# A decoder layer with attention, a selective scan and a ternary feed-forward: row sums broadcast through memory, quantisation from centred values, and new order tables

## The chip, the cores and the metric

One core of a Trainium2 chip runs the whole layer in one launch. The metric is the device time of that launch in microseconds. Engines are PE (TensorE), DVE (VectorE), ACT (ScalarE), POOL (GpSimd) and SP (SyncE, which here only issues DMAs).

## The reference, cut to what matters

Four sequences (B = 4) of L = 512 rows and DM = 512 columns pass through three residual blocks; all is float32.

```
x = x + attention(layernorm(x))             # 16 heads of 32, rotary, causal softmax, w_o
x = x + ssm(ctx, z = layernorm(x))          # conv, silu, selective scan with 16 states, gate silu(z)
x = x + ffn(layernorm(x))                   # bitlinear, gelu, bitlinear

bitlinear(x, w):  xn = (x - mean(x)) / sqrt(var(x) + EPS)
                  gamma = max(abs(xn))                      # per row
                  x_hat = clip(xn * 128 / gamma, -128, 128) * gamma / 128
                  w_hat = sign(round(w / mean(abs(w)))) * mean(abs(w))
                  return x_hat @ w_hat.T
softmax: exp(scores - rowmax) / rowsum
ssm:     state = state * exp(delta * A) + delta * u * B_t ;  y_t = sum_n state * C_t
         delta = softplus(dt_proj(dt_lo) + bias)
```

Two facts of this matter below. Dividing a row by its own largest absolute value gives the same quotient whether or not the row was first multiplied by a positive number per row. And the softmax's row sum is one number per query row and head, while the product with V stands with the query rows along the free dimension, so the reciprocals must be spread over the 32 partitions of their head.

## The kernel before, in words

**Tiling.** A sequence is cut into 4 blocks of 128 rows, its channels into 4 blocks of 128 partitions. Attention runs in 32 slots (`p`), one for two heads of one sequence: `s` (scores, PE), its row maxima (DVE), `e` (exponentials with the row sums in `z_sum`, ACT, line 1487), `t` (transposes, PE, copies by ACT at 1503). Two slots make a group `g` of four heads, 16 groups in all: `rz` (reciprocals of the row sums) and `pv` (product with V, PE, line 1694). Line 1908 on DVE multiplies the product in PSUM with `rz_t` and writes `o_t`, from which `wo`, the output projection, is made.

**The row sums before.** DVE takes the reciprocal of 128 x 16 values (line 1900). PE multiplies each column, broadcast to 32 columns, with the identity, 16 products of 128 x 128, each of them two passes as the profile counts them (line 1731), into a bank of PSUM. ACT copies the bank to `rz_t` (line 1510). DVE's multiply at 1908 waits for that copy.

**The scan.** For each sequence and each of 16 states, ACT makes the factors (line 1377), POOL the inputs from `du` and `b_bc` (line 1248), DVE scans along the rows (lines 1795, 1803), PE transposes the result (line 1708) and DVE adds it into `y_acc` (line 1817). `b_bc` is a row of B_t broadcast to 128 partitions, loaded by SP (lines 1166, 1167) from `bc_d` in memory, two buffers. `delta` is a softplus: ACT computes relu, abs, exp and log into one scratch tile `tmp` (lines 1455 to 1461); then four instructions read it, on DVE for sequence 0 (lines 1857 to 1863), on POOL for the others (from line 1259). ACT waits with a block until the `delta` of the block before is made.

**The feed-forward.** 16 tiles of 128 rows. `xa` (statistics on DVE; on POOL six small instructions, lines 1309 to 1319, that give mean, reciprocal deviation and their product with a second deviation), `xc` (DVE subtracts the mean and multiplies with the gain, line 1985, takes the largest absolute value, 1987, and its reciprocal, 1989; POOL scales, 1325), `xt` (transposes into a high and a low part), `fc` (matmuls, line 1766, gelu by ACT, 1546, statistics by DVE, 2012), `hstat` (DVE's aggregate, 2017; three POOL instructions, 1334 to 1338), `hn` (ACT centres and scales two halves, line 1565, DVE takes their maxima, 2022), `hscale`, `hq` (DVE scales, 2035), `ht_ffn` (transposes, 1757; the low part by DVE, 2007), `proj` (line 1775) and DVE's `y_out` (2042). The tiles begin while the last sequence is still being scanned.

**What sets the order.** Each engine executes its list in order and waits on semaphores. The lists come from `plan()`, a planner that runs before the kernel is written. It takes due times for each item from tables (`STATE`, `ATTN`, `FRONT`, `TILE`, `PACE` and others), adds a weight for each engine and kind (`WEIGHT`), and with costs and needs from `follows()` picks, for the engine that can start first, the ready item that is due first. SP is one such engine, so loads and stores have one order too. It also places PSUM banks and puts transposes of no use into PE's list where PE would wait (`FILLS`, line 1582). A change of a table moves instructions on all engines.

**The start.** SP loads two blocks of x, the identity and small constants, ctx of sequence 0 with `in_w` behind it, then the residual of sequence 0 (`xr`, 1 MB, line 1189), and further loads of x. The chunks 0 and 1 of `w_ring` follow, with the rotary tables behind the first and the scan weights `xp_w` and `dt_w` behind the second.

## Time and profile before

| | |
|---|---|
| median of 3 runs | 1136.7 us (1135.46 to 1136.88) |
| the profiled execution: time, span | 1134.5 us, 1132.7 us |
| mean granted TensorE clock | 0.953 of full |
| PE busy | 1003.6 us (89%), 6034 instructions |
| DVE busy | 958.9 us (85%), 1351 |
| ACT busy | 793.3 us (70%), 1529 |
| POOL busy | 625.1 us (55%), 509 |
| DMA queue | 114.7 MB, 32.4% of 16 engines |

Busy time counts an instruction's execution, not its waits. PE's includes the fill transposes. Row forms are: `L1731 PE MATMUL out<-in shapes xcount | busy us, mean ns | idle before, with the releasers` for a group, and `engine line <- releaser: us in total, times, longest us` for a wait. SPq is the issuing of DMAs by SP. A time in a list "in order of time" is in us from the start of the span, followed by the duration.

### The profile page before, as it was taken

The page shows a single profiled execution, that of the slowest core. Times are in us where ns is not written, and L with a number is a line of the kernel's source. Part 1 is how long each engine was busy: PE and PEld are TensorE (multiplying, and loading weights), DVE is VectorE, ACT ScalarE, POOL GpSimd, SP SyncE. Part 2 cuts the span into 40 slices and gives each one's busy share as a digit, 9 for nine tenths or more (in the row PEclk, how much of TensorE's full clock was granted, in tenths as well). Part 3 has the DMA queues.
Part 4 walks back from the last instruction along what each step waited for, and adds up shares of the span by engine and source line. Part 5 has one row for each costly group of instructions (what it writes and reads, how often), then busy time and mean ns, then how long its engine had stood idle before and what let it go on. Part 6 is the DMA issues. An engine that isn't in the chain of part 4 may idle for free. (4 is left out here: it accounts for less than half of the span.)

```text
span 1132.7 us, 18945 instructions
## 1 busy us (share of the span) xinstructions
PE 1003.6 (89%) x6034; PEld 760.6 (67%) x6034; DVE 958.9 (85%) x1351; ACT 793.3 (70%) x1529; POOL 625.1 (55%) x509
## 2 busy tenths in 40 slices
PE   7998988999988999789899985887888998989997
PEld 5555666669664668556567664676767776878886
DVE  5758898996998869998986789899999999998654
ACT  4656756765786776888767696827988978984432
POOL 1369485554536796456738831569655655544401
PEclk9999999999988999899999986997899999989999
DMA  5325356364435545323555460420111110000000
GB/s 194 114 76 171 109 151 184 105 198 152 116 103 182 154 131 168 103 81 106 167 190 159 139 194 6 175 105 26 41 47 34 38 33 32 26 16 19 10 19 19
DMA packets 59360, 115.91 MB, mean 102 GB/s; under 512 B 8880, under 2 KB 13232, under 8 KB 58240
## 3 DMA queue, kind: packets, MB, share of 16 engines
q1 hardware_dynamic: 59264, 114.70, 32.4%
q8 instruction: 51, 0.84, 0.3%
q14 instruction: 45, 0.37, 0.1%
HBM read 90.42 MB, written 24.25 MB: 101 GB/s over the span
## 5 line engine op out<-in xcount | busy, mean ns | idle before, releaser
L1248 POOL TENSOR_TENSOR hb<-du,b_bc 128x1024 f32<-128x1024 f32 (+1 forms) x160 | 314.8, 1987 | 160.6 <-PE ps L1708 160.6
L1795 DVE TENSOR_TENSOR_SCAN hb<-ps,hb 128x1024 f32<-128x1024 f32 (+1 forms) x128 | 257.4, 2013 | 33.3 <-ACT ps L1377 20.0
L1377 ACT ACTIVATE ps<-delta,a_neg 128x511 f32<-128x511 f32 (+2 forms) x320 | 180.6, 600 | 79.5 <-DVE hb L1795 73.3
L1817 DVE SCALAR_TENSOR_TENSOR y_acc<-ps,ct,y_acc 128x512 f32<-128x512 f32 x256 | 181.2, 740 | 24.5 <-PE ps L1708 23.8
L1708 PE MATMUL ps<-ident,hb 128*128 128x128 f32 x1088 | 160.1, 288 | 43.8 <-DVE hb L1795 12.7
L1708 PEld LDWEIGHTS ps<-ident,hb 128*128 128x128 f32 x1088 | 127.8, 147 | 72.1 <-issue 14.2
L1487 ACT ACTIVATE p_q<-ps,m_col 128x512 f32<-128x512 f32 (+3 forms) x256 | 131.5, 530 | 20.9 <-DVE m_col L1892 12.2
L1639 PE MATMUL ps<-xn_t,w_ring 128*128 128x512 f32 x256 | 117.9, 604 | 0.8 <-DVE o_t L1908 0.6
L1766 PE MATMUL ps<-t_fc,xq_hi 128*128 128x512 f32 x256 | 106.2, 415 | 3.2 <-DVE hq_lo L2007 3.2
L1682 PE MATMUL ps<-ident,p_q 128*128 128x128 f32 x640 | 91.9, 287 | 14.4 <-ACT p_q L1487 7.2
L1503 ACT ACTIVATE p_t<-ps 128x512 f32<-128x512 f32 x160 | 88.2, 605 | 22.9 <-PE ps L1682 22.6
L1775 PE MATMUL ps<-t_pr,hq_hi 128*128 128x512 f32 x256 | 102.2, 399 | 1.9 <-DVE hq_lo L2007 1.9
L1766 PE MATMUL ps<-t_fc,xq_lo 128*128 128x512 f32 x256 | 101.9, 398 | 0.0
L1775 PE MATMUL ps<-t_pr,hq_lo 128*128 128x512 f32 x256 | 101.1, 395 | 0.0
L1892 DVE TENSOR_REDUCE m_col<-ps 128x1 f32<-128x512 f32 (+2 forms) x192 | 88.5, 501 | 8.1 <-PE ps L1667 7.0
L1682 PEld LDWEIGHTS ps<-ident,p_q 128*128 128x128 f32 x640 | 75.0, 147 | 28.5 <-ACT p_q L1487 9.2
L1663 PE MATMUL ps<-k_st,q_st 128*128 128x512 f32 (+3 forms) x256 | 76.5, 374 | 10.5 <-DVE y_acc L1817 7.8
L1639 PEld LDWEIGHTS ps<-xn_t,w_ring 128*128 128x128 f32 x256 | 46.9, 192 | 52.5 <-issue 50.0
L1582 PE MATMUL ps<-ident 128*128 128x128 f32 x478 | 67.4, 292 | 11.2 <-DMA small<-in_small 5.5
L1582 PEld LDWEIGHTS ps<-ident 128*128 128x128 f32 x478 | 59.1, 152 | 18.0 <-DMA small<-in_small 5.5
L1546 ACT ACTIVATE h_sb<-ps,fx 128x512 f32<-128x512 f32 x64 | 42.7, 686 | 30.1 <-PE ps L1766 28.5
L1565 ACT ACTIVATE h_sb<-h_sb,fh 128x1024 f32<-128x1024 f32 x32 | 38.4, 1236 | 30.9 <-POOL fh L1338 30.9
(151 smaller groups left out, 2016.5 us busy)
## 6 DMA issues: line engine op xcount, KB each, us to landing
w_ring<-in_w_attn SPq DMA_DIRECT2D x32, 512.0 KB, 3.7
qk_d<-hl SPq DMA_DIRECT2D x64, 256.0 KB
q_st<-qk_d SPq DMA_DIRECT2D x128, 128.0 KB, 2.8
b_bc<-bc_d SPq DMA_DIRECT2D x48, 256.0 KB, 3.9
k_st<-qk_d SPq DMA_DIRECT2D x64, 128.0 KB, 2.7
k_st<-qk_d SPq DMA_DIRECT2D x128, 64.0 KB, 2.3
x_in<-in_x SPq DMA_DIRECT2D x16, 256.0 KB, 2.9
raw_fc<-in_w_fc SPq DMA_DIRECT2D x4, 1024.0 KB, 9.2
```

What stands on the lines that cost most here:

```text
L1248: nc.gpsimd.tensor_tensor(piece_of(e, hi, lo).rearrange("p (a n) -> p a n", a=2), du[b % 2][:, 2 * h:2 * h + 2, lo:hi], b_bc[:, i % BC_RIN ...
L1377: ins = nc.scalar.activation(factors(j, hi, lo)[:, (hi - lo) * m + start:(hi - lo) * (m + 1)], delta[b % 2][:, et, lo + start:hi], ACT.Exp ...
L1487: ins = nc.scalar.activation(p_q[:, h, Q_AT[i]:Q_AT[i] + w], src[:, col:col + w], ACT.Exp, bias=m_col[:, i, h:h + 1], accum_out=z_sum[:, b ...
L1582: nc.tensor.transpose(bank(*item)[:, 0:P], ident[:], ident[:])
L1639: mm = nc.tensor.matmul(bank(kind, *a), w_ring[:, c % 2, d, P * half:P * half + P], xn_t[:, d, :], start=(d == 0), stop=(d == KD - 1))
L1682: mm = nc.tensor.transpose(dst[:, at:at + P], p_q[:, h, Q_AT[i] + P * jt:Q_AT[i] + P * jt + P], ident[:])
L1708: mm = nc.tensor.transpose(bank(kind, *a)[:, P * et:P * et + P], piece_of(2 * r + et // 2, hi, lo)[:, at:at + P], ident[:])
L1766: mm = nc.tensor.matmul(bank(kind, t, n), part[:, t % 2, d, :], t_fc[:, d, 512 * n:512 * n + 512], start=(d == 0 and m == 0), stop=(d == K ...
L1775: mm = nc.tensor.matmul(bank(kind, t), part[:, k, :], t_pr[:, k, :], start=(k == 0 and m == 0), stop=(k == FT - 1 and m == 1))
L1795: v.tensor_tensor_scan(h, d, h, 0.0, ALU.mult, ALU.add).then_inc(scan_done, 1)
L1817: v.scalar_tensor_tensor(out=y, in0=bank(kind, r, tb), scalar=ct[:, b % 2, tb, n:n + 1], in1=y, op0=ALU.mult, op1=ALU.add).then_inc(y_free ...
L1892: ins = v.tensor_reduce(m_col[:, i, h:h + 1], src[:, col:col + P * (i + 1)], AX.X, ALU.max, negate=True)
```

## The change

Five things are changed.

1. **Row sums.** PE's matmuls and ACT's copy for `rz` are removed. After DVE's reciprocal SP stores the 128 x 16 values to memory in another order, `[row block, head, row]`, and then loads them back into `rz_t` with four loads, each broadcast to 32 partitions. DVE's multiply waits for the loads. The planner has a due time of its own for `rzload`.
2. **Quantisation.** `xc` only subtracts the mean and takes maximum and reciprocal of the centred values; the gain goes into the scale that POOL computes for the gelu. `hn` on ACT only negates and centres (mean minus value, scale -1); the gain with a minus sign goes into the scale for `y_out`. Neither waits for POOL's gain any longer; POOL's scale instructions do.
3. **Scratch.** In sequence 0 the softplus of odd blocks uses `gate` in place of `tmp`, so each block waits for the `delta` of two blocks before.
4. **Loads.** The scan weights are loaded behind `in_w`; the first residual stands after the store of `x_dbl`.
5. **Tables.** Due times and weights for all engines are new.

```diff
 ATTN = {'stack': [-11.6],
  's': [-0.6, 1.0, 2.6, 4.2, 5.8],
- 'e': [1.2, 2.8, 4.4, 6, 7.6],
- 't': [8.4, 9.6, 9.6, 10.8, 12.0],
+ 'e': [1.2, 2.8, 4.4, 6.2, 7.8],
+ 't': [8.4, 9.6, 9.6, 9.8, 11.0],
  'pv': [14.6]}
 
...
-LAST_STATE = {'exp': [-4.8, -1.8], 'dbu': [-8.0, -5.0], 'scan': [0.9, 3], 'carry': [3.0, 6.0], 'ht': [4.6, 5.8]}
...
+LAST_STATE = {'exp': [-4.7, -1.7], 'dbu': [-8.3, -5.0], 'scan': [0.9, 3], 'carry': [11.0, 14.0], 'ht': [4.6, 5.8]}
...
-QUOTIENT = {'rz': [11.4]}
+QUOTIENT = {'rz': [21.2], 'rzload': [13.6]}
...
-PACE = {'slot': 18.0, 'ffn': 597.2, 'tile': 15, 'tail': 835.1, 'tail_step': 6.4, 'tail_load': -19.6}
...
+PACE = {'slot': 18.0, 'ffn': 597.2, 'tile': 15.5, 'tail': 822.6, 'tail_step': 13.6, 'tail_load': -18.7}
...
+def scratch_user(b, et):
+
+
+    i = ET * b + et
+    return None if i < 2 else divmod(i - 2 if b == 0 else i - 1, ET)
...
     elif kind == "xproj":
...
-        yield "pe", 3.5, [act("silu", b, ET - 1), sp("wload", 1)]
+        yield "pe", 3.5, [act("silu", b, ET - 1), sp("cload", 0)]
...
     elif kind == "e":
-        yield "act", 1.3, [dve("s", *a)] + ([pe("t", a[0] - 1, 4)] if a[0] else [])
+        p, n = a
+        yield "act", 1.3, [dve("s", *a)] + ([pe("t", p - 1, 4)] if p else []) + ([sp("rz", p // 2 - 8)] if p >= 16 else [])
...
-        yield "dve", 0.7, [pe(*item), act("rz", g)] + ([pe("wo", b - 1, 1, 1)] if b else [])
+        yield "dve", 0.7, [pe(*item), sp("rzload", g)] + ([pe("wo", b - 1, 1, 1)] if b else [])
     elif kind == "rz":
...
-        yield "pe", 0.5, [dve(*item)]
-        yield "act", 0.6, [pe(*item)] + ([dve("pv", g - 1)] if g else [])
+        yield "sp", 1.5, [dve(*item)]
+    elif kind == "rzload":
+        g, = a
+        yield "sp", 1.0, [sp("rz", g)] + ([dve("pv", g - 1)] if g else [])
     elif kind == "resid":
...
-            [pe("pv", SLOTS // 2 - 1)] if b else []
+            [pe("pv", SLOTS // 2 - 1)] if b else [sp("xproj", 0)]
...
     elif kind == "xc":
...
-        yield "dve", 1.9, [pool("xa", t), pe("xt", t - 2) if t >= 2 else dve("wo", B - 1, 1, 1)]
-        yield "pool", 1.5, [dve(*item), dve("wtot", 0)] + ([act("fc", t - 4, 3)] if t >= 4 else [])
+        yield "dve", 1.9, [dve("xa", t), pe("xt", t - 2) if t >= 2 else dve("wo", B - 1, 1, 1)]
+        yield "pool", 1.5, [dve(*item), pool("xa", t), dve("wtot", 0)] + ([act("fc", t - 4, 3)] if t >= 4 else [])
...
     elif kind == "hstat":
-        yield "dve", 0.35, [dve("fc", *a, 3)]
-        yield "pool", 1.1, [dve(*item)]
+        yield "dve", 0.35, [dve("fc", *a, 3)] + ([pool("hstat", a[0] - 4)] if a[0] >= 4 else [])
+        yield "pool", 1.1, [dve(*item), dve("wtot", 1)]
     elif kind == "hn":
-        yield "act", 1.3, [pool("hstat", a[0])]
+        yield "act", 1.3, [dve("hstat", a[0])]
...
     elif kind == "hscale":
...
-        yield "pool", 0.3, [dve(*item), dve("wtot", 1)]
+        yield "pool", 0.3, [dve(*item), pool("hstat", *a)]
...
-            before["pe", item] = before["pe", item] + [x for who in readers for x in before[who, item] if x[1] != item and (x[0], x[1][:2]) != ("pe", ("fc", item[1]))]
+            before["pe", item] = before["pe", item] + [x for who in readers for x in before[who, item] if x[1] != item and x[1][0] != "rzload" and (x[0], x[1][:2]) != ("pe", ("fc", item[1]))]
...
-        if engine == "pe" and item[0] == "dt" and scratch:
-            if scratch[-1] not in over:
+        if engine == "pe" and item[0] == "dt" and scratch_user(*item[1:]):
+            user = scratch_user(*item[1:])
+            made = delta_by(user[0]), ("delta", *user)
+            if made not in over:
...
-            at = max(at, over[scratch[-1]])
+            at = max(at, over[made])
...
-                    if c < 2:
-                        load_consts(("rotary", "scan")[c])
+                    if c == 0:
+                        load_consts("rotary")
...
+                        load_consts("scan")
...
+                elif kind == "rz":
+                    g, = a
+                    sp.wait_ge(z_ready, g + 1)
+                    sp.dma_start(rz_d[g].rearrange("i q p -> p (i q)"), z_sum[:, g // 4 % 2, g % 4].rearrange("p i q -> p (i q)"),
+                                 allow_slow_non_contiguous=True)\
+                        .then_inc(rz_stored, 16)
+                elif kind == "rzload":
+                    g, = a
+                    sp.wait_ge(rz_stored, 16 * (g + 1))
+                    if g:
+                        emptied(sp, TASK["pv", g - 1])
+                    for quad in range(4):
+                        sp.dma_start(rz_t[HD * quad:HD * quad + HD, :].rearrange("d (i p) -> d i p", p=P),
+                                     rz_d[g, :, quad].partition_broadcast(HD)).then_inc(rz_in, 16)
...
-                    nc.gpsimd.tensor_scalar(f[:, 7:8], f[:, 2:3], f[:, 3:4], None, ALU.mult).then_inc(fx_pow, 1)
+                    nc.gpsimd.tensor_scalar(f[:, 7:8], f[:, 2:3], f[:, 3:4], None, ALU.mult).then_inc(fx_gain, 1)
...
-                    nc.gpsimd.tensor_scalar(f[:, 12:13], f[:, 8:9], gam[:, 0:1], None, ALU.mult).then_inc(fx_scale, 1)
+                    pool.wait_ge(fx_gain, t + 1)
+                    nc.gpsimd.tensor_scalar(f[:, 12:13], f[:, 8:9], f[:, 7:8], gam[:, 0:1], ALU.mult, ALU.mult).then_inc(fx_scale, 1)
...
-                    nc.gpsimd.tensor_scalar(f[:, 3:4], f[:, 0:1], f[:, 2:3], -1.0, ALU.mult, ALU.mult).then_inc(fh_nmr, 1)
+                    pool.wait_ge(gam_ready, 2)
+                    nc.gpsimd.tensor_scalar(f[:, 3:4], f[:, 2:3], gam[:, 1:2], -1.0, ALU.mult, ALU.mult).then_inc(fh_gain, 1)
                 elif kind == "hscale":
...
-                    pool.wait_ge(gam_ready, 2)
-                    nc.gpsimd.tensor_scalar(f[:, 12:13], f[:, 8:9], gam[:, 1:2], None, ALU.mult).then_inc(fh_scale, 1)
+                    pool.wait_ge(fh_gain, t + 1)
+                    nc.gpsimd.tensor_scalar(f[:, 12:13], f[:, 8:9], f[:, 3:4], None, ALU.mult).then_inc(fh_scale, 1)
...
-                    if b or et:
-                        delta_made(act, *divmod(ET * b + et - 1, ET))
-                    nc.scalar.activation(tmp[:, 0, :], bank(kind, *a), ACT.Relu, bias=dt_b[:, et, :])
-                    nc.scalar.activation(tmp[:, 1, :], bank(kind, *a), ACT.Abs, bias=dt_b[:, et, :])\
+                    if scratch_user(b, et):
+                        delta_made(act, *scratch_user(b, et))
+                    s = scratch(b, et)
+                    nc.scalar.activation(s[:, 0, :], bank(kind, *a), ACT.Relu, bias=dt_b[:, et, :])
+                    nc.scalar.activation(s[:, 1, :], bank(kind, *a), ACT.Abs, bias=dt_b[:, et, :])\
...
-                    own.done(nc.scalar.activation(tmp[:, 1, :], tmp[:, 1, :], ACT.Exp, scale=-1.0))
-                    own.settle()
-                    nc.scalar.activation(tmp[:, 2, :], tmp[:, 1, :], ACT.Ln, bias=1.0).then_inc(sp_ready, 1)
+                    own.done(nc.scalar.activation(s[:, 1, :], s[:, 1, :], ACT.Exp, scale=-1.0))
+                    own.settle()
+                    nc.scalar.activation(s[:, 2, :], s[:, 1, :], ACT.Ln, bias=1.0).then_inc(sp_ready, 1)
...
+                    if b >= 2:
+                        act.wait_ge(rz_stored, 16 * (p // 2 - 7))
...
-                elif kind == "rz":
-
-                    g, = a
-                    act.wait_ge(m_full, TASK[kind, g] + 1)
-                    if g:
-                        emptied(act, TASK["pv", g - 1])
-                    nc.scalar.activation(rz_t[:], bank(kind, g), ACT.Copy).then_inc(m_free["act"], 1)
...
                 elif kind == "hn":
...
-                    act.wait_ge(fh_nmr, t + 1)
+                    act.wait_ge(fh_var, t + 1)
...
-                    nc.scalar.activation(half, half, ACT.Identity, bias=fh[:, t % 4, 3:4],
-                                         scale=fh[:, t % 4, 2:3]).then_inc(hn_done, 1)
+                    nc.scalar.activation(half, half, ACT.Identity, bias=fh[:, t % 4, 0:1], scale=-1.0).then_inc(hn_done, 1)
...
-                elif kind == "rz":
-
-                    g, = a
-                    pe.wait_ge(z_ready, g + 1)
-                    for i in range(LT):
-                        for quad in range(4):
-                            z = z_sum[:, g // 4 % 2, g % 4, i, quad:quad + 1].to_broadcast([P, HD])
-                            mm = nc.tensor.matmul(bank(kind, g)[HD * quad:HD * quad + HD, P * i:P * i + P], z, ident[:],
-                                                  start=True, stop=True)
-                    mm.then_inc(m_full, 1)
...
-                    d = delta[b % 2][:, et, :]
-                    own.done(v.tensor_scalar(d, tmp[:, 1, :], 1.0, 1.0, ALU.add, ALU.subtract))
-                    own.settle()
-                    own.done(v.tensor_tensor(d, tmp[:, 1, :], d, ALU.subtract))
-                    own.settle()
-                    own.done(v.tensor_tensor(d, d, tmp[:, 2, :], ALU.add))
-                    own.settle()
-                    v.tensor_tensor(d, d, tmp[:, 0, :], ALU.add).then_inc(delta_ready["dve"], 1)
+                    d, s = delta[b % 2][:, et, :], scratch(b, et)
+                    own.done(v.tensor_scalar(d, s[:, 1, :], 1.0, 1.0, ALU.add, ALU.subtract))
+                    own.settle()
+                    own.done(v.tensor_tensor(d, s[:, 1, :], d, ALU.subtract))
+                    own.settle()
+                    own.done(v.tensor_tensor(d, d, s[:, 2, :], ALU.add))
+                    own.settle()
+                    v.tensor_tensor(d, d, s[:, 0, :], ALU.add).then_inc(delta_ready["dve"], 1)
...
-                    emptied(dve, TASK["rz", g])
+                    dve.wait_ge(rz_in, 64 * (g + 1))
...
+                    if t >= 4:
+                        dve.wait_ge(fx_gain, t - 3)
...
                 elif kind == "xc":
...
-                    dve.wait_ge(fx_pow, t + 1)
...
-                    own.done(v.tensor_scalar(x, x2(t), f[:, 0:1], f[:, 7:8], ALU.subtract, ALU.mult))
+                    dve.wait_ge(fx_var, t + 1)
+                    own.done(v.tensor_scalar(x, x2(t), f[:, 0:1], None, ALU.subtract))
...
+                    if t >= 4:
+                        dve.wait_ge(fh_gain, t - 3)
```

Of the tables (some 100 changed numbers) only a few stand here.

## Rows read from the trace of the kernel before

**Rows 1.** stretch, us, busy PE PEld DVE ACT POOL (instructions), PEclk, DMA share, GB/s:

```profile
100.00:640.00 540.00, 492.18 (x3252) 355.36 (x3252) 464.09 (x621) 392.22 (x883) 333.46 (x190) 0.97 0.46 140
...
760.00:1000.00 240.00, 209.60 (x1073) 174.13 (x1073) 231.80 (x366) 203.18 (x303) 146.15 (x179) 0.94 0.11 33
1000.00:1060.00 60.00, 55.59 (x277) 46.36 (x276) 52.40 (x93) 32.12 (x45) 33.09 (x52) 0.94 0.04 14
1060.00:1100.00 40.00, 40.00 (x199) 33.33 (x198) 22.23 (x35) 15.49 (x23) 4.91 (x8) 1.00 0.05 21
```

**Rows 2.** the same for PE's fill transposes of line 1582 alone:

```profile
100.00:740.00 640.00, 27.88 (x200) 23.40 (x200) 0.95 0.46 141
```

**Rows 3.** groups of the page's kind: busy, mean ns, idle before and its releasers:

```profile
L1731 PE MATMUL ps<-ident,z_sum 128*32 128x128 f32 x512 | 18.4, 287 | 4.8 <-DVE z_sum L1900 3.8 <-DVE y_acc L1817 0.8
...
L1510 ACT ACTIVATE rz_t<-ps 128x512 f32<-128x512 f32 x16 | 9.6, 600 | 12.1 <-PE ps L1731 12.1
```

**Rows 4.** DMA issues (KB each, us to landing), three issues of SP:

```profile
k_st<-qk_d SPq DMA_DIRECT2D x128, 64.0 KB, 2.3
...
bc_d<-x_dbl SPq DMA_DIRECT2D x4, 32.0 KB, 2.2
...
510.43 1.70 SPq L1181 DMA_DIRECT2D k_st<-qk_d  x3
```

**Rows 5.** DMA packets and queue share, 3.5:4 us, then 36:39.2 us:

```profile
DMA packets 174, 0.07 MB, mean 149 GB/s; under 512 B 96, under 2 KB 170, under 8 KB 174
...
q1 hardware_dynamic: 174, 0.07, 83.2%
...
DMA packets 32, 0.03 MB, mean 10 GB/s; under 512 B 16, under 2 KB 16, under 8 KB 32
...
q1 hardware_dynamic: 32, 0.03, 4.7%
```

**Rows 6.** DVE in order of time: start, duration, what:

```profile
308.62 0.24 DVE L1900 RECIPROCAL z_sum<-z_sum 128x16 f32<-128x16 f32 x1
...
320.14 0.68 DVE L1908 TENSOR_TENSOR o_t<-ps,rz_t 128x512 f32<-128x512 f32 x1
...
643.47 0.24 DVE L1900 RECIPROCAL z_sum<-z_sum 128x16 f32<-128x16 f32 x1
...
650.29 0.69 DVE L1908 TENSOR_TENSOR o_t<-ps,rz_t 128x512 f32<-128x512 f32 x1 [2.12 <-PE ps L1694]
```

**Rows 7.** who waited for tile o_t's multiply: us, times:

```profile
  PE ps L1708: 9.6, 2
...
  PE ps L1682: 0.2, 1
```

**Rows 8.** the chain that ended last, in order of time, near the end:

```profile
1071.10 7.46 PE ps L1775 x32
...
1098.10 0.28 DVE fh L2017
...
1099.71 1.25 ACT h_sb L1565
```

**Rows 9.** waits from 760 to 1000 us: us in total, times, longest:

```profile
ACT h_sb L1565 <- POOL fh L1338: 10.3, 7, 2.3
```

**Rows 10.** the head in order of time:

```profile
3.52 0.43 SPq L1189 DMA_DIRECT2D xr<-in_x  x1
11.97 0.98 SPq L1134 DMA_DIRECT2D x_in<-in_x  x2
...
44.13 0.49 DVE L1857 TENSOR_SCALAR delta<-tmp 128x512 f32<-128x512 f32 x1 [2.38 <-ACT tmp L1461]
...
48.92 0.69 ACT L1455 ACTIVATE tmp<-ps,small 128x512 f32<-128x512 f32 x1 [0.89 <-DVE delta L1863]
```

**Rows 11.** waits over the whole span: us in total, times, longest:

```profile
DVE delta L1857 <- ACT tmp L1461: 4.4, 3, 2.4
...
SPq L1166 <- POOL hb L1248: 294.2, 47, 20.7
```

178 lines of the change are left out of this document (92 added, 86 removed), and 2 rows, old and new, of the table ATTN_END.

## The prediction, made before the changed kernel ran

> **What bounds the kernel now.** I read the busy time by stretch first; the reader should see that no engine is the bound everywhere. From 100 to 640 us (attention and scans) PE has 492.2 of 540 us, DVE 464.1: 91% and 86%, level once PE's fill transposes are taken off (27.9 us from 100 to 740) [rows 1, 2]. From 760 to 1000 us (last scans and FFN tiles) DVE has 231.8 of 240 us, 97%, and PE 87%: DVE bounds there. From 1060 to 1100 PE is busy all the time [rows 1], and after that two tiles end one behind the other. So a saving on PE counts before 740 us and after 1060 us, and one on waits of DVE counts between, up to DVE's idle time there: 8.2 us from 760 to 1000 and 7.6 us from 1000 to 1060 [rows 1].
>
> I then read the groups of the lines that the diff touches, and the order of time of the reciprocal and of the multiply that uses it, because what was an engine's work becomes a round trip through memory.
>
> **Part 1, the broadcast leaves PE and ACT.** Line 1731 is 512 instructions, 18.4 us of PE, and PE waited 3.8 us for the reciprocal before it; line 1510 is 16 copies, 9.6 us of ACT, and ACT waited 12.1 us for PE there [rows 3]. ACT is busy 73% of the stretch from 100 to 640 us [rows 1], so its 9.6 us are taken at nothing; the work that hides them is PE's and DVE's own. PE's 18.4 + 3.8 = 22.2 us are worth between nothing (the planner puts fills where PE waits, and DVE is as loaded) and all. I take half, as two engines of nearly equal load share the path: -11.1 us. A bank of PSUM is also held 16 times fewer; nothing shows a price for that.
>
> **Part 2, the round trip.** In its place: a reciprocal on DVE, SP's wait, a store of 128 x 16 values of 4 bytes each to scattered addresses, SP's wait for it, four loads of 64 KB written to 32 partitions each, and only then DVE's multiply at line 1908. DVE executes in order, so a late load stops scans, maxima and y_acc behind it. The reciprocal takes 0.24 us (its row stands with the gaps below). A store of 32 KB with the 16 rows of bc_d lands after 2.2 us. SP issues three loads of k_st in 1.70 us, 0.57 each, so the fourth starts 1.7 us after the first, and such a load lands 2.3 us after its issue [rows 4]. Without a price for small pieces the trip is 0.24 + 2.2 + 1.7 + 2.3 = 6.4 us. The store has 2048 pieces, 128 for each of 16 DMA engines. No row shows 4-byte data. Two rows bound a packet: the stretch with mostly small packets has 174 in 83.2% of 16 x 0.5 us, 38 ns each; the one with 2 KB packets and completion writes has 32 in 4.7% of 16 x 3.2 us, 75 ns each [rows 5]. So 128 packets add 0, 4.9 or 9.6 us, and the trip takes 6.4, 11.3 or 16.0 us. I take 11.3, the row of small packets being nearest.
>
> The Trainium skill (DMA: Bandwidth & Descriptors, Rules for kernel authors) says that a strided last dimension lowers to one descriptor per element and advises to rearrange it, which speaks against this store. The Trainium skill (same page, Bandwidth) gives about 10.5 ns per packet for a 4 KB transfer; by that, as an estimate, the store would add 1.3 us, not 4.9, and the trip would be 7.7 us. The trace has nothing of that kind, so the sum does not use it.
>
> How much time is there? Between the reciprocal and the multiply the 16 groups have 7.2, 8.4, 8.9, 11.0, 42.9, 11.5, 17.2, 17.9, 18.3, 8.2, 8.4, 9.0, 35.0, 6.8, 16.6 and 8.6 us, from the start of the one to the start of the other; the shortest and the tenth shortest of the 16 stand as rows [rows 6]. Ten are under 12 us and add up to 88.0. A trip of 11.3 us overruns nine of them (76.5 in sum) by 9 x 11.3 - 76.5 = 25 us; one of 6.4 us none; one of 16.0 us all ten by 72 us. Not every stall reaches the end: PE waited for the old multiply in 7 of 16 cases (six rows by line, the first of 2 cases and the last of 1 stand here) [rows 7], so I take 0.4: +10.0 us, with ends 0 and +29 (or +36, if half passes on). The tables move the reciprocal's due time, and the new order may open or shut these gaps; I leave them as they are.
>
> **Part 3, quantisation from centred values.** No instruction goes. The chain on GpSimd (variance plus epsilon, power, product) no longer stands ahead of line 1565, which waits for DVE's aggregate alone. In the tail this is seen in the chain of waits: the aggregate ends at 1098.38 and the centring starts at 1099.71 us, so 1.3 us go [rows 8]. What is late next is the same ACT pass. The other tail tile has its chain beside the projection before it: nothing. In the middle ACT waited 10.3 us for GpSimd at line 1565 between 760 and 1000 us [rows 9], but that is idle time of an engine which isn't the bound; DVE there has only 8.2 us of idle time, and half of it, -4.1, is what I take, with ends 0 and the full 8.2 + 7.6 = 15.8. For line 1985 DVE waited for no such chain in a listed row, so that edit costs and brings nothing by itself; the added waits on fx_gain and fh_gain are for tiles four back, hidden by the tiles between. The scale for y_out now waits for the gain, and has the projection's 7.5 us as cover [rows 8].
>
> **Part 4, the head.** A second scratch for batch 0 lets ACT start a block's softplus before DVE has read the one before. ACT waited 0.89 us for that at 48.92, DVE's delta waited 2.38 us for ACT at 44.13 [rows 10]. I take -2.0, with ends 0 and -4.4 (all that DVE waited at line 1857) [rows 11]. The first residual, 1 MB, was issued at 3.52 us, behind the activations and in_w; SP's next load, x_in at 11.97 us [rows 10], waits for PE's transposes, not for that transfer. So its removal from the head gives nothing, and the load, put after the x_dbl store, has over 100 us until the output projection of batch 0 needs it. xp_w and dt_w go from behind the second load of w_ring to behind in_w: two issues of 0.43 us as the others there, and what is behind them on SP, x_in of block 2, is held by PE anyway. Nothing, with ends -1 and +1.
>
> **Part 5, new tables.** They reorder all five engines. Nothing in the trace of before prices an order that it doesn't show; I take 0, with -10 and +10 as ends, the order of PE's waits that remain.
>
> **The sum.** -11.1 + 10.0 - 1.3 - 4.1 - 2.0 = -8.5 us. The profiled execution took 1134.5 us, so 1126.0; it stands 2.2 us under the median of the runs, and 1136.7 - 8.5 gives 1128.2, say 1128. A difference of 0.2%, 2.3 us, is about what a measurement of this kernel can tell from none.
>
> **The rivals.** *The round trip comes late (slower).* Place: DVE at line 1908. If the store's packets cost 75 ns, the overrun is 72 us, and with half of it passed on +36; the other terms are -11.1 - 1.3 - 4.1 - 2.0 = -18.5, so +17.5, 1154 us. At 0.4 it decides once the overrun passes 18.5 / 0.4 = 46 us; since ten gaps overrun by 10R - 88, from a trip of 13.4 us on. For it: the short gaps, and a first row of 2048 tiny pieces. Against it: packets of 38 ns. The Trainium skill's rule on strided last dimensions (DMA: Bandwidth & Descriptors, Rules for kernel authors) is on its side. Chance 0.20.
>
> *SP comes late (slower).* SP executes in order too, and stood 294 us in 47 waits, up to 20.7, at the loads of b_bc, which wait for GpSimd [rows 11]. A reciprocal stored behind such a wait, 6.3 us on average, meets it perhaps one time in two: the trip is 14.4 us, the overrun 56, 0.4 of it 22, less 18.5: +4, 1141; where it is every time, 17.6 us and 88, +17, 1154. Middle 1146. Against it: the planner places the store by its own due time. Chance 0.10.
>
> *All of it is on the path (much faster).* -22.2 - 1.3 - 15.8 - 4.4 = -43.7, 1093 us, if the trip fits its gaps. For it: PE's 91%. Against it: DVE's 86% beside it, and 97% later. Chance 0.18, mostly in its upper half, 1095 to 1118.
>
> *No change.* PE's freed time fills with fills or with waits for DVE, which gets nothing less to do; stalls pay back the tail: 1135 to 1139. Chance 0.12. That the change does not do what it says is not among these: each removed instruction is gone from the code.
>
> The forecast, a moderate gain between 1119 and 1134, has 0.40. Faster than 0.2%: 0.40 + 0.18 = 0.58. Same: 0.12. Slower: 0.20 + 0.10 = 0.30. The range from 1104 to 1152 leaves out the lower part of the full gain and the top of the two late cases, about 2 in 10.
>
> **What would show it.** Right: no rows of lines 1731 and 1510; the store landing in 6 to 8 us; a wait of DVE at the multiply for rz_t of some 1 to 3 us in about half of 16 cases; DVE still above 95% from 760 to 1000; the aggregate and the centring of the last tiles 0.1 us apart; PE's busy time down by 18 us less what fills take. Wrong: a store that lands in 3 us (then nothing stalls, and the gain is nearer 18), stalls over 45 us in sum, SP's wait ahead of the store, or a stretch of 100 to 740 us that changes by more than 15 us for another reason: then the order, not the pieces, decided.

## The result and the profile after: 1175.7 us, slower by 3.6%

The changed kernel takes 1175.7 us in the median (1175.18 to 1180.46, 4 runs), the kernel before 1136.6 in the same runs: a ratio of 1.0357 [1.0336, 1.0378], 39 us slower. The forecast of 1128, its range (1104 to 1152) and its sign were wrong. The profiled execution has a span of 1173.4 us and a mean granted clock of 0.94 (0.953 before).

The stretches that answer to three of the four lines of [rows 1], in the same form:

```profile
100.00:640.00 540.00, 463.03 (x2600) 326.83 (x2599) 424.01 (x564) 362.94 (x804) 296.76 (x169) 0.93 0.57 137
760.00:1000.00 240.00, 200.19 (x1130) 167.34 (x1128) 223.61 (x334) 182.69 (x295) 151.33 (x171) 0.96 0.19 53
...
1060.00:1100.00 40.00, 39.23 (x206) 32.85 (x205) 32.91 (x56) 16.07 (x26) 11.79 (x18) 1.00 0.05 20
```

From 100 to 640 us PE went from 492.2 to 463.0 us and DVE from 464.1 to 424.0; ACT and POOL lost busy time too. All four have less to do in the same stretch: the whole machine is held up by something that is none of them. The DMA share rose from 0.46 to 0.57 while the rate fell from 140 to 137 GB/s. Time is lost before 800 us: the last multiply with the row sums starts at 788.0 us, in the kernel before at 733.4. Of these 54.6 us the rest of the kernel gives 14 back, since the span grew by 40.7.

DMA packets and their queue:

```profile
DMA packets 101597, 120.18 MB, mean 102 GB/s; under 512 B 42928, under 2 KB 55472, under 8 KB 100480
...
q1 hardware_dynamic: 101504, 119.04, 39.6%
```

The kernel before has 59360 packets, 8880 of them under 512 B, and a queue share of 32.4%. The added 34048 small packets are 16 x 2048 = 32768 pieces of the stores and 1280 others, 16 for each of the 80 added DMAs. So each store is 2048 packets, and the Trainium skill's rule on a strided last dimension (DMA: Bandwidth & Descriptors, Rules for kernel authors) agrees with the trace.

The chain that ended last, by engine and by line, then the same in order of time from 128 to 161 us:

```profile
PE 42%; DVE 17%; DMA 12%; POOL 9%; issue 8%; SPq 7%; ACT 4%; DVEq 0%; POOLq 0%; ACTq 0%
PE ps L1797 9%; DMA rz_d<-z_sum 7%; PE ps L1671 6%; PE ps L1788 6%; PE ps L1740 5%; SPq L1202 4%; DVE hb L1817 4%; POOL hb L1283 3%; DVE y_acc L1839 3%; PE ps L1684 3%; PE ps L1714 3%; DMA rz_t<-rz_d 2%; PE ps L1752 2%; PE ps L1779 2%; PE ps L1645 1%
```

```profile
128.98 0.63 SPq L1177
...
131.15 1.74 SPq L1177
...
132.93 11.72 DMA rz_d<-z_sum
144.67 0.33 SPq L1215
...
146.00 3.11 DMA rz_t<-rz_d
...
149.19 0.09 DVE o_t L1930
...
149.80 0.25 DVE z_sum L1922
150.07 10.93 DMA rz_d<-z_sum
161.02 0.31 SPq L1215
```

The chain runs through the store (11.7 us), SP's four loads, their landing, the multiply, and then the next store (10.9 us). DMA has 12% of the chain. DVE and then SP in order of time show where the trip begins:

```profile
126.85 0.25 DVE L1922 RECIPROCAL z_sum<-z_sum 128x16 f32<-128x16 f32 x1 [2.60 <-ACT p_q L1527]
...
149.19 0.69 DVE L1930 TENSOR_TENSOR o_t<-ps,rz_t 128x512 f32<-128x512 f32 x1 [3.46 <-DMA rz_t<-rz_d]
```

```profile
126.79 1.69 SPq L1202 DMA_DIRECT2D k_st<-qk_d  x3
128.57 0.37 SPq L1188 DMA_DIRECT2D b_bc<-bc_d  x1
128.98 3.91 SPq L1177 DMA_DIRECT2D qk_d<-hl  x4
132.93 1.31 SPq L1206 DMA_DIRECT2D rz_d<-z_sum  x1
144.67 1.75 SPq L1215 DMA_DIRECT2D rz_t<-rz_d  x4
```

SP takes 6.1 us to come to the store, because it is issuing other DMAs, and then stands 10.4 us between the end of the store's issue and the first load, with its own list behind it. From the reciprocal to the multiply it is 22.3 us (126.85 to 149.19). In 8 of the 16 groups SP stands still until the store has landed; there the loads start 10.9 to 13.5 us after the store's issue. SP's own waits for the store:

```profile
SPq L1215 <- DMA rz_d<-z_sum: 67.3, 8, 10.8
```

The waits of the other engines (us in total, times, longest):

```profile
DVE y_acc L1839 <- PE ps L1740: 35.0, 25, 4.1
DVE o_t L1930 <- DMA rz_t<-rz_d: 33.6, 10, 6.0
...
POOL hb L1283 <- DMA b_bc<-bc_d: 17.5, 4, 6.2
DVE stats L1846 <- DMA x_in<-in_x: 17.1, 4, 7.1
```

The kernel before has 23.8, none, none and 1.4 us in their places. The last two are waits for loads that have nothing to do with row sums; e3 shows which of them goes with the store. While a store runs, a load of weights issued behind it (151 to 160 us, with the packets) looks like this:

```profile
DMA packets 2126, 0.26 MB, mean 29 GB/s; under 512 B 2064, under 2 KB 2064, under 8 KB 2126
...
q1 hardware_dynamic: 2126, 0.26, 69.6%
...
w_ring<-in_w_attn SPq DMA_DIRECT2D x1, 512.0 KB, 13.0
```

The 16 DMA engines are 69.6% busy and move 29 GB/s in all, and the load lands after 13.0 us. Of the 32 loads of `w_ring` 7 take over 8 us to land, the longest 13.4; in the kernel before none takes over 6.4, and the median is 3.7.

### The profile page after: what moved, and what is told of

Same layout as the page of the kernel before. It is cut to its first block, busy times and chain, and to the rows that moved or that the text cites. A ratio compares the mean times of both kernels' runs of the same rounds, so it can differ in the third digit from the quotient of the medians.

```text
span 1173.4 us, 18082 instructions
## 1 busy us (share of the span) xinstructions
PE 1010.8 (86%) x5560; PEld 765.4 (65%) x5560; DVE 959.5 (82%) x1351; ACT 786.2 (67%) x1517; POOL 629.1 (54%) x509
## 2 busy tenths in 40 slices
DMA packets 101597, 120.18 MB, mean 102 GB/s; under 512 B 42928, under 2 KB 55472, under 8 KB 100480
## 4 chain that ended last, share of the span: by engine, by line
PE 42%; DVE 17%; DMA 12%; POOL 9%; issue 8%; SPq 7%; ACT 4%; DVEq 0%; POOLq 0%; ACTq 0%
PE ps L1797 9%; DMA rz_d<-z_sum 7%; PE ps L1671 6%; PE ps L1788 6%; PE ps L1740 5%; SPq L1202 4%; DVE hb L1817 4%; POOL hb L1283 3%; DVE y_acc L1839 3%; PE ps L1684 3%; PE ps L1714 3%; DMA rz_t<-rz_d 2%; PE ps L1752 2%; PE ps L1779 2%; PE ps L1645 1%
## 5 line engine op out<-in xcount | busy, mean ns | idle before, releaser
L1283 POOL TENSOR_TENSOR hb<-du,b_bc 128x1024 f32<-128x1024 f32 (+1 forms) x160 | 308.4, 1947 | 180.0 <-PE ps L1740 162.4
L1740 PEld LDWEIGHTS ps<-ident,hb 128*128 128x128 f32 x1088 | 130.5, 149 | 90.7 <-issue 38.8
L1671 PE MATMUL ps<-xn_t,w_ring 128*128 128x512 f32 x256 | 125.5, 636 | 5.6 <-DVE hl L1895 4.2
L1714 PE MATMUL ps<-ident,p_q 128*128 128x128 f32 x640 | 94.7, 296 | 21.3 <-ACT p_t L1543 7.1
L1714 PEld LDWEIGHTS ps<-ident,p_q 128*128 128x128 f32 x640 | 79.0, 153 | 38.1 <-ACT p_t L1543 9.9
L1914 DVE TENSOR_REDUCE m_col<-ps 128x1 f32<-128x512 f32 (+2 forms) x192 | 88.7, 502 | 17.3 <-PE ps L1699 10.2
L1671 PEld LDWEIGHTS ps<-xn_t,w_ring 128*128 128x128 f32 x256 | 49.8, 205 | 62.5 <-issue 54.8
L1614 PE MATMUL ps<-ident 128*128 128x128 f32 x516 | 73.2, 294 | 9.1 <-DMA small<-in_small 5.7
L1614 PEld LDWEIGHTS ps<-ident 128*128 128x128 f32 x516 | 65.1, 153 | 14.5 <-DMA small<-in_small 5.7
L1695 PEld LDWEIGHTS ps<-k_st,q_st 128*128 128x128 f32 x256 | 45.2, 208 | 44.9 <-DVE y_acc L1839 27.3
L1314 POOL TENSOR_TENSOR hl<-hl 128x512 f32<-128x512 f32 x16 | 20.4, 1273 | 100.8 <-DVE hl L1902 100.6
```

Source lines behind the costliest of these rows:

```text
L1283: nc.gpsimd.tensor_tensor(piece_of(e, hi, lo).rearrange("p (a n) -> p a n", a=2), du[b % 2][:, 2 * h:2 * h + 2, lo:hi], b_bc[:, i % BC_RIN ...
L1614: nc.tensor.transpose(bank(*item)[:, 0:P], ident[:], ident[:])
L1671: mm = nc.tensor.matmul(bank(kind, *a), w_ring[:, c % 2, d, P * half:P * half + P], xn_t[:, d, :], start=(d == 0), stop=(d == KD - 1))
L1695: nc.tensor.matmul(dst[:, col:col + w], q_st[:, p % 2, h, P * i:P * i + P], k_st[:, p % 2, h, 0:w], start=(u == 0), stop=False)
L1714: mm = nc.tensor.transpose(dst[:, at:at + P], p_q[:, h, Q_AT[i] + P * jt:Q_AT[i] + P * jt + P], ident[:])
L1740: mm = nc.tensor.transpose(bank(kind, *a)[:, P * et:P * et + P], piece_of(2 * r + et // 2, hi, lo)[:, at:at + P], ident[:])
```

## The experiments

Each is the changed kernel or the kernel before with the edit named, timed beside the kernel before (1135 to 1136 us). The edits are shown cut, and in part told in words. "Tables" are the planner's due times and weights. Parts are numbered as in the prediction.

### e1: the row sums stay on PE, all else as changed

```
-   "rz": sp store, "rzload": sp loads, DVE waits for rz_in
+   "rz": 16 matmuls on PE, a copy by ACT, DVE waits for the copy
-QUOTIENT = {'rz': [21.2], 'rzload': [13.6]}
+QUOTIENT = {'rz': [11.4]}
 (and the two weights of rz as before)
```

> The changed kernel with the row sums as before (PE matmuls, ACT copy, rz due 11.4 with the weights of before); all else, the new tables too, as changed. Theory A, the round trip through memory costs the time: 1125 to 1140 us, attention over near 735 us. Rival B, the new tables cost it: 1160 us or more with no DMA wait at the multiply. Rival C, both: about 1150.

1171.5 us (1166.65 to 1176.39), 1.0302 [1.0253, 1.0351]. Without the trip the changed kernel is nearly as slow as with it. Taken alone this is what rival B expected: the tables, not the trip. Either the rest of the change costs 35 us, or the new tables don't suit a kernel whose sums are on PE; e3 and e9 tell.

### e2: the trip alone, in the kernel before

```
+   "rz": sp store, "rzload": sp loads, as in the change
-QUOTIENT = {'rz': [11.4]}
+QUOTIENT = {'rz': [11.4], 'rzload': [13.6]}
```

> The kernel before with only the row sums sent through memory (rz due 11.4, rzload due 13.6); tables, loads, scratch and quantisation as before. Theory A: 1165 to 1190 us, the store landing 11 us or more after its issue and DVE waiting 30 us or more in sum at the multiply. Rival B: within 10 us of before, 1136 to 1147.

1226.0 us, 1.0788 [1.0743, 1.0833]: the trip alone, on the old tables, costs 90 us, more than theory A's 1165 to 1190. DVE waits 32.0 us for `rz_t` in 9 cases and POOL 31.4 us for `b_bc` in 4, up to 14.9. As in the changed kernel, the wait at the multiply is only a part of it.

### e3: the store in whole rows of 64 bytes

```
-sp.dma_start(rz_d[g].rearrange("i q p -> p (i q)"), z_sum[...],
-             allow_slow_non_contiguous=True)
+sp.dma_start(rz_d[g].rearrange("i q p -> (i q p)").rearrange("(p c) -> p c", c=16), z_sum[...])
```

It leaves out the reordering of the row sums: each stores its 16 values side by side, so the loads fetch others than they should. Everything else is the changed kernel, instruction by instruction.

> The changed kernel with the store written as 128 rows of 64 bytes in place of 2048 pieces of 4 bytes. The values then stand in another order than the loads expect, so the reordering is what it leaves out; instructions, waits and number of DMAs are the same. If the small pieces are the cost (A): the store lands in 2 to 3 us and the time falls to 1125 to 1145. If it is the trip as such, SP's order and two DMA latencies (D): 1155 to 1175.

1131.2 us, 0.9949 [0.9927, 0.997]. One access pattern is worth 44 us. Issues (KB each, us to landing), then two waits, then the stretch from 100 to 640 us, in which PE's and DVE's busy times come back towards those of the kernel before:

```profile
w_ring<-in_w_attn SPq DMA_DIRECT2D x32, 512.0 KB, 3.8
...
rz_d<-z_sum SPq DMA_DIRECT2D x16, 8.0 KB, 3.5
```

```profile
DVE stats L1846 <- DMA x_in<-in_x: 16.1, 4, 8.3
...
DVE o_t L1930 <- DMA rz_t<-rz_d: 3.9, 2, 2.5
```

```profile
100.00:640.00 540.00, 487.62 (x2840) 348.61 (x2839) 450.42 (x604) 390.21 (x864) 328.29 (x187) 0.97 0.50 150
```

The store lands in 3.5 us in the median, and of 33.6 us of waits at the multiply 3.9 are left; POOL's wait for `b_bc` falls from 17.5 to 5.6 us. The wait for `x_in` is nearly as long as in the changed kernel (17.1 us), so it is no part of the 44 us.

Something else changed with the store. PE executes 5560 matmul instructions in both kernels:

```profile
PE 1010.8 (86%) x5560; PEld 765.4 (65%) x5560; DVE 959.5 (82%) x1351; ACT 786.2 (67%) x1517; POOL 629.1 (54%) x509
...
PE 992.3 (88%) x5560; PEld 753.1 (67%) x5560; DVE 954.6 (85%) x1351; ACT 785.7 (70%) x1517; POOL 628.6 (56%) x509
```

The first line is the changed kernel's, with a mean granted clock of 0.93 from 100 to 640 us, the second e3's, with 0.97. So PE is busy 18.5 us longer for the same instructions. How much of the 44 us goes through this lower clock, and how much is waiting alone, no run separates.

### e4: centred quantisation alone, in the kernel before

```
-act: activation(half, Identity, bias=fh[3:4], scale=fh[2:3])   # waits for POOL's chain
+act: activation(half, Identity, bias=fh[0:1], scale=-1.0)      # waits for DVE's aggregate
+pool: xc and hscale multiply by the deviations as well; xa, xc the same way
```

> The kernel before with only the quantisation from centred values, tables as before. By my steps 1.3 us in the tail and half of DVE's idle time in the middle: 1131 us, range 1120 to 1136. Rival: the plan with other needs shifts the order and eats it, 1136 to 1145.

1138.1 us, 1.001 [0.9988, 1.0031]: no difference that can be told from none, where the prediction had -5.4.

### e5: the trip alone, with the store in whole rows

```
 e2 with the store of e3
```

> The kernel of e2 (tables of before, row sums through memory) with the store of whole rows of e3; it leaves out the reordering of the values in the same way. If small pieces and tables add up: e2 falls by the 45 us that e3 gained, to about 1180 us, and the new tables are worth some 50 us to a kernel with the trip. If the pieces are all of it: 1130 to 1145 us, and the tables only made the stalls of the small pieces less bad.

1167.0 us, 1.0287 [1.0268, 1.0307]. The pieces cost 59 us here (1226.0 less 1167.0) and 44 under the new tables. The run lies between the two results that were expected (1180, or 1130 to 1145). Even a trip of short transfers costs 32 us on the tables of before, and with the new tables and the rest of the change it stands 5 us under the kernel before. Yet DVE waits only 0.2 us for `rz_t` here, in one case. So the 32 us are not a wait for the trip: they arise through the order that the planner makes with it. Which part of the order holds them isn't shown.

### e6: e3 with the store of pieces beside it, and nobody waiting for it

```
 (store in whole rows, four loads)
+sp.dma_start(rx_d[g].rearrange("i q p -> p (i q)"), z_sum[...],
+             allow_slow_non_contiguous=True).then_inc(rx_stored, 16)
```

Like e3, e5 and e11 it leaves out the reordering of the row sums in what the loads read. The pieces go to another array that nothing reads. SP issues them behind the loads; the reuse of `z_sum` two sequences later waits for them.

> e3 with a second store for each group, of the 2048 small pieces to a memory of its own, issued behind the four loads; nothing waits for it but the sums of two sequences later and the kernel's end. It tells the store's latency at the multiply from its blocking of the queue. If the latency is the cost: 1131 to 1140 us. If the queue behind it is the cost (everything that SP issues in the next 10 us lands late): 1155 to 1175 us, and loads of w_ring, b_bc and x_in behind it land in 10 us or more.

1165.2 us, 1.0264 [1.0237, 1.029], 34 us above e3, though DVE waits 3.3 us in all for `rz_t` (3.9 in e3). Issues of e6:

```profile
w_ring<-in_w_attn SPq DMA_DIRECT2D x32, 512.0 KB, 5.4
...
b_bc<-bc_d SPq DMA_DIRECT2D x48, 256.0 KB, 5.2
```

Both landed in 3.8 us in e3. The median is less than the 10 us that were expected, but single loads are held long: 7 of the 32 of `w_ring` and 14 of the 80 of `b_bc` take over 8 us, none and 1 in e3. So a cost of 34 us, against the 44, arises with nobody waiting for the store but the reuse of `z_sum`: the store holds the other transfers. That it is the pieces, and not one more DMA in SP's list, no run with a second store of whole rows shows directly; but e7, with three more stores in each group, is only 2 us above e3. This holding was not in the prediction at all.

### e7: the values turned on DVE before the store

```
-v.reciprocal(z, z).then_inc(z_ready, 1)
+own.done(v.reciprocal(z, z)); own.settle()
+v.transpose(zt[:], z_all[:, 16 * (g % 8):16 * (g % 8) + 32]).then_inc(z_ready, 1)
-(one store of 2048 pieces)
+for n in range(4):
+    sp.dma_start(rz_d[g, :, :, 32 * n:32 * n + 32].rearrange("i q p -> (i q) p"),
+                 zt[32 * n + 16:32 * n + 32, :]).then_inc(rz_stored, 16)
```

> The changed kernel, but DVE turns the reciprocals in blocks of 32 x 32 before the store, and the store is four DMAs of 16 rows of 128 bytes, 64 pieces in place of 2048; all of the layer is computed, the order of each engine's items is unchanged. If the small pieces are the cause: 1128 to 1138 us, some 3 us of that over e3 for three more issues on SP; the stores land in 2 to 3 us. If another property of e3 made it fast: over 1150 us.

1133.3 us (12 runs), 0.999 [0.9971, 1.001]. A 32 x 32 transpose in blocks puts 32 rows side by side, so each of four stores has 16 pieces of 128 bytes; they land in 2.2 us. DVE waits with each reciprocal until the stores of the group before have landed. This kernel computes the whole layer and gives back 42 us of the 44.

### e8: the planner told what the store takes

```
-        yield "sp", 1.5, [dve(*item)]
+        yield "sp", 11, [dve(*item)]
-rz_stored = sem("rz_stored")
+rz_stored = [sem("rz_stored0"), sem("rz_stored1")]
```

> The changed kernel with its small pieces, but the planner is told that the store takes 11 us on SP's line in place of 1.5, with two semaphores for the store. If the loss is one of an order made for the wrong cost: DVE's wait at the multiply goes from 33.6 us to under 10, and 1140 to 1160 us. If the blocked queue is the loss whatever the order: 1165 to 1185 us.

1272.6 us, 1.1228 [1.1193, 1.1263], far above both ranges that were expected. The cost in the planner is SP's issuing, so SP now counts as taken for 11 us and what stands behind it is planned late. No trace of an execution of this length was kept; what exactly grew stays open. It doesn't test whether a planner that knew the landing apart from the issue would help.

### e9: all edits of the code but the row sums, with the tables of before

```
 kernel before
+centred quantisation, second scratch array (gate), scan weights with in_w,
+first residual behind the first xproj transfer
```

> The kernel before with all code changes but the row sums (centred values, second scratch, order of the loads), and the tables of before. e1 had the same code with the new tables and took 1171 us. If the new tables don't fit a kernel with PE sums: 1128 to 1142 us here. If the scratch or the loads cost the 35 us of e1: 1160 us or more.

1159.3 us, 1.0207 [1.0167, 1.0247]. Parts 3 and 4 together cost 23 us on the old tables. The prediction had -7.4. DVE waits 16.7 us for `x_in` in 4 cases, 1.4 before. Whether that wait is the cost isn't shown by this run, so the parts were tried singly: e13, e14, e15. The only difference from e1 is the tables: with the new ones the same code takes 12 us more (1171.5).

### e10: one due time of the kernel before moved by 1 us

```
-QUOTIENT = {'rz': [11.4]}
+QUOTIENT = {'rz': [12.4]}
```

> The kernel before with a single number of its tables changed, the due time of rz from 11.4 to 12.4. It tells how much an order found for one kernel is worth against an arbitrary neighbour. If the order matters little: within 5 us of before. If tables and code must fit each other closely: 1145 to 1170 us.

1138.6 us, 1.0024 [1.0006, 1.0043]. One due time makes 2.7 us: the order is sensitive, but a single small step doesn't cost tens of microseconds.

### e11: the unwaited pieces of e6 on ACT's queue

```
-sp.dma_start(rx_d[g]..., z_sum[...])
+nc.scalar.dma_start(rx_d[g]..., z_sum[...])   # 15 of 16 groups, behind a copy of the next slot
```

> e6 (whole rows for the sums, and a second store of 2048 small pieces that nothing waits for), but the second store is issued by ACT, on ACT's queue, after a copy of the next slot; 15 of 16 groups have it, the orders are the same. If only SP's own queue is held: 1131 to 1145 us, DMAs of SP landing as in e3. If the small pieces hold the DMA engines or what feeds them for all queues: 1155 to 1175 us, as e6.

1167.9 us, 1.0267 [1.0232, 1.0303], as e6. Another engine's queue doesn't shield SP's loads: `b_bc` lands in 5.5 us (over 8 us in 15 of 80), and `hl` and the multiply wait 9.9 and 12.3 us for SP's transfers (0.8 and 3.9 in e3). Each issue takes ACT 0.4 us, under 6 us in all, so it isn't ACT's time that costs 37. The Trainium skill (DMA: Bandwidth & Descriptors, Issuing engines are not separate DMA queues) says that DMAs of all issuing engines run on the same 16 engines and interleave; e11 agrees with it, 37 us above e3 where a queue of its own would have given e3's 1131.

### e12: pieces of 8 bytes, 1024 of them

```
-sp.dma_start(rz_d[g].rearrange("i q p -> p (i q)"), z_sum...rearrange("p i q -> p (i q)"),
+sp.dma_start(rz_d[g].rearrange("i q p -> (i q p)").rearrange("(c p e) -> p c e", p=P, e=2),
+             z_sum...rearrange("p i q -> p (i q)").rearrange("p (c e) -> p c e", e=2),
```

It too leaves out the full reordering of the row sums.

> The changed kernel with the store in 1024 pieces of 8 bytes in place of 2048 of 4 (the values land in another order than the loads expect; all else the same). If the cost goes by the number of pieces: the store lands after some 6 us, and the time is about half way between e3 and the changed kernel, 1143 to 1158 us. If it goes by something else (a read and a write of each small piece in memory, or a limit under some size): as the changed kernel, 1170 or more, or as e3, under 1136.

1136.2 us, 1.0011 [0.9991, 1.0032]. Issues, then DVE's wait:

```profile
w_ring<-in_w_attn SPq DMA_DIRECT2D x32, 512.0 KB, 4.2
...
rz_d<-z_sum SPq DMA_DIRECT2D x16, 8.0 KB, 5.7
```

```profile
DVE o_t L1931 <- DMA rz_t<-rz_d: 9.2, 5, 4.4
```

Pieces per store, landing and time: 128, 3.5 us, 1131; 1024, 5.7 us, 1136; 2048, about 11 us, 1176. The first 896 pieces cost 5 us of the kernel, the next 1024 cost 40. By the number of pieces 1143 to 1158 us had been expected: the landing came as expected (some 6 us), the time did not. Probably a landing under 6 us still fits the gaps that the order leaves; DVE's wait at the multiply, 9.2 us against 3.9 and 33.6, speaks for it, but no run tests it.

### e13, e14, e15: the edits of part 4 one at a time, in the kernel before

```
 e13  own.done(... tmp ...)  ->  scratch(b, et): gate if b == 0 and et % 2 else tmp
 e14  load_consts(("rotary", "scan")[c])  ->  load_consts("inproj"); load_consts("scan")
 e15  resid:  [] if not b  ->  [sp("xproj", 0)] if not b
```

> The kernel before with one edit of part 4: every other tile of the first sequence works delta in the array of the gate, and the planner counts its uses so. The kernel before with all edits of the code but the sums took 1159.3 us, 23 us above the kernel before, and centred quantisation alone 1138.1. Theory A (the 21 us come from the moved loads: x_in comes late behind them): 1136 +-3, and DVE waits for x_in about 1.4 us as before. Theory B (they come from the second scratch array, through the order that the planner makes of the head): 1150 to 1159. Theory C (the old tables fit the old code alone, and every edit that the planner sees costs a part): 1142 to 1148.

1143.9 us, 1.0067 [1.0046, 1.0087].

> The kernel before with one edit of part 4: the scan's constants are loaded with those of the input projection, ahead of the second load of weights, not behind it. Theory A (moved loads cost the 21 us): either this run or that of the residual takes 1150 to 1159, with DVE waiting over 10 us for x_in. Theory B (the scratch array): 1136 +-3. Theory C (every edit costs a part): 1140 to 1148.

1133.5 us, 0.998 [0.9964, 0.9995].

> The kernel before with one edit of part 4: the load of the first residual waits in the planner for the first xproj transfer. Theory A (moved loads cost the 21 us): this run or that of the scan's constants takes 1150 to 1159, with DVE waiting over 10 us for x_in. Theory B (the scratch array): 1136 +-3. Theory C (every edit costs a part): 1140 to 1148.

1147.5 us, 1.0095 [1.0062, 1.0128]. Against the 1135.9 us of these runs: +8.0, -2.4, +11.5. With e4's +2.2 (1138.1 less 1135.9) they add up to +19.3; e9 has +23. No single one holds the loss, and the residual's and the scratch array's times are in theory C's ranges; the scan's load, which by C would cost too, gains 2.4 us and is in no theory's range, so C holds for two of three. The late wait for `x_in` goes with the residual's edit (these lines are e15's):

```profile
DVE y_acc L1817 <- PE ps L1708: 39.6, 29, 8.9
...
DVE stats L1824 <- DMA x_in<-in_x: 15.4, 4, 7.5
```

and in e13, without it, that wait is 1.4 us as before.

### e16, e17: two of these edits undone under the new tables

```
 e16  e7 with the first residual in the place of before
 e17  e7 with the one scratch array of before
```

> The changed kernel with the row sums turned on DVE before the store (1133.3 us, 0.999 of the kernel before) and the first residual back in the place of before, the new tables kept. Theory C (a set of tables fits the code that it was made with, whatever the edit is worth by itself): slower than 1133, 1137 to 1150. Theory D (the later residual costs 11 us by itself, as it did with the old tables): 1122 to 1128, which would be below both kernels.

1140.8 us, 1.0039 [1.002, 1.0058], 7 us above e7 (6 by the ratios), though DVE's wait for `x_in` falls from 17.3 to 5.8 us. So that wait doesn't measure what the edit costs.

> The same kernel of 1133.3 us with the second scratch array taken back, the new tables kept. Theory C (tables fit their code): 1137 to 1150. Theory D (the array costs 8 us by itself, as it did with the old tables): 1124 to 1130.

1132.4 us, 0.9966 [0.9948, 0.9984], level with e7, in neither theory's range. The residual's edit costs 11.5 us under the old tables, and taking it back costs 7 under the new ones. So it is neither good nor bad by itself: it goes with its tables. The scratch array costs 8 us under the old tables and nothing either way under the new ones, so not every edit depends on its tables in both directions. e17 computes the whole and is 0.3% below the kernel before; among seventeen variants that is a small lead. Nothing here that computes the whole beats the kernel before by more.

## Why the prediction was wrong

**Part 2, the size of a piece.** "I take 11.3, the row of small packets being nearest": this step failed first. The row chosen gave 38 ns a packet. The store lands after 10.9 us at the least, and less the 2.2 us of the comparison store that is 8.7 / 128 = 68 ns. The other bound, 75 ns, was nearly right. Of the packets in the 38 ns row 96 of 174 were under 512 B, but nothing showed that any was as small as 4 bytes. From the reciprocal to the landing of the last load the trip takes 15.3 us in the shortest group and over 18 in all others; 11.3 is reached in none. The estimate by the Trainium skill's figure of about 10.5 ns per packet (DMA: Bandwidth & Descriptors, Bandwidth), 1.3 us for the store's pieces, is far below the same 8.7 us. It was also worked out wrongly: the page divides the 0.67 us of one 4 KB transfer by all its 64 packets, and the prediction multiplied the result with the 128 pieces of a single engine. With all 2048 pieces it would be, as an estimate, 21.5 us, far above the measurement.

**Part 2, what the store holds.** The sum priced the trip by DVE's wait at the multiply alone. That wait is 33.6 us in 10 cases, where 25 in nine were predicted, but the nearness is luck: two errors cancel. By the prediction's own 10R - 88 a trip of 15.3 us would already overrun by 65 us. And the gaps between reciprocal and multiply, taken from the trace of before and left "as they are", didn't stay. In e3, where DVE waits only 3.9 us for the loads, they add up to 373 us with 12.9 us as the shortest, against 236 and 6.8 before; in the changed kernel the shortest is 19.0:

```profile
505.63 0.24 DVE L1922 RECIPROCAL z_sum<-z_sum 128x16 f32<-128x16 f32 x1
...
524.61 0.69 DVE L1930 TENSOR_TENSOR o_t<-ps,rz_t 128x512 f32<-128x512 f32 x1 [5.91 <-DMA rz_t<-rz_d]
```

Passed on at 0.4, the 33.6 us are 13, and even in full they are less than the 44 that the pieces cost (e3 against the changed kernel). The term that was missing is the DMA engines' time: while the store runs, for some 11 us, 16 times, other transfers land late (`w_ring` after up to 13.4 us, before up to 6.3), and the engines that wait for them pass it on. e6 gives it: 34 us with nobody waiting for the store. e11 shows that a second issuing engine doesn't remove it.

**The rivals.** "The round trip comes late" was right in its place and its sign, with a turning point (a trip of 13.4 us) that was passed in every group. Its 1154 was 22 us too low, and the missing term is in none of its parts. "SP comes late" came true in part, at another place than named: in the first group 6.1 us behind SP's own issues of `k_st`, `b_bc` and `qk_d`, not behind the wait for `b_bc`'s buffer; in the 16 groups the store's issue starts 3.4 us after the reciprocal on average. The two were priced as alternatives, but they add: 6.1 + 11.7 + the loads.

**Part 1.** -11.1 for the matmuls taken from PE can't be read singly, since no run has the change without the trip and with tables made for it. Together with the short trip, the other parts and the new tables it is worth 5 us (e3). The prediction had -18.5 for all but the trip; what part of the 13 us between them a short trip costs, and what part was never there, isn't shown.

**Part 3.** -5.4 us predicted, +0.1% [-0.12, +0.31] measured (e4). The half of DVE's idle time from 760 to 1000 us isn't there: DVE idles 10.9 us in that stretch of e4, 8.2 in the kernel before. ACT had waited for that chain, and its wait at the centring falls from 10.3 to 3.2 us without a gain. The tail's 1.3 us did go: in the changed kernel's last tile the centring starts 0.04 us after the aggregate's end (1152.39 and 1152.35). But that is within the measurement's error.

**Parts 4 and 5.** "Nothing, with ends -1 and +1" for the loads and -2.0 for the scratch array left out the planner. It plans all five engines from these edits, and with the old tables they make +8.0 us (scratch array), -2.4 (scan weights) and +11.5 (residual). And 0 with ends of 10 for the tables was undersized: e1 less e9, the same code under new and old tables, is +12 us. Tables and code go together: e1 stands 35 us above the kernel before with new tables and old sums, e5 32 us above it the other way round, and each together with its own partner lands within 5 us of 1136. The prediction said that the new order may open or shut the gaps ("I leave them as they are") and drew no width from it.

Of the signs of being wrong that the prediction named, "SP's wait ahead of the store" came true as lateness (up to 8.7 us; in the first group spent issuing, not waiting), and so did a stretch from 100 to 740 us that changes by more than 15 us (DVE's busy time there falls from 549.8 to 506.5). But the reading that the prediction gave to this, "then the order, not the pieces, decided", did not: with the order kept, e3 takes the loss away. The stalls at the multiply stayed under 45 us. Of its signs of being right, that of the last tiles came, and the two lines are gone. But the store landed after 10.9 us and more, not 6 to 8; DVE waited 3.4 us on average at the multiply, not 1 to 3; DVE is at 93% from 760 to 1000 us, not above 95; and PE's busy time rose by 7 us, while 18 less than before had been expected (in e3 it fell by 11).

**What stays open.** How the 44 us divide beyond e6's 34; the rest, 10, is what waiting for the store adds (DVE at the multiply, and SP, which waits 67.3 us for the store and 9.7 in e3), if the two don't overlap. How much of both is PE's lower clock. Which transfer held up which engine in e6: its waits grow by a few us each over e3's (DVE's for `x_in` from 16.1 to 22.4), and none of them alone is near 34. Why e8's order is so poor, and e5's with a trip that nobody waits for.

## What to carry to other kernels

Price a DMA by its number of pieces and charge it to the other transfers in flight too, not only to whoever waits for it: here 2048 pieces of 4 bytes took 11 us, in which the 16 DMA engines moved little else, and issuing them from ACT in place of SP gained nothing (e6, e11). Values spread over partitions are better turned on an engine first (here by one transpose in 32 x 32 blocks on DVE) and stored in rows, here of 128 bytes. And where a planner makes the order, measure an edit together with tables made for it: here new tables with old sums, or a short trip with old tables, cost 32 to 35 us that no matched pair showed.

## What the runs showed of the hardware that was not expected

- The landing of a store isn't proportional to its pieces: 3.5 us for 128 of 64 bytes, 5.7 for 1024 of 8 (both medians), about 11 for 2048 of 4 (the chain's two, 11.7 and 10.9). From the second to the third that is 5.3 us for 64 more pieces per engine, 83 ns each, against 39 ns from the first to the second (2.2 us for 56). The size of a piece changed with the number, and other transfers ran beside, so these runs don't tell which of them bends the line.
- During such a store the 16 engines show 69.6% busy at 29 GB/s, so a high DMA share doesn't tell that much data moves. The count of packets under 512 B (42928 against 8880) shows the cause at once.
- The time of this kernel is far from linear in the landing: 2.2 us more cost 5 us, the next 5.3 us cost 40.
